# Edge pass of a graph network kernel: sixteen unread products a step in an unused PSUM bank

## The reference, cut to what matters

```
gate = silu(edge_attr @ F1W + F1b) @ F2W + F2b
ei = emb[atom_z[src]]
ej = emb[atom_z[dst]]
gate = gate + (ei * (ej @ adapt)).sum(-1, keepdims=True)
cw = where(distances < CUT, 0.5 * (cos(pi * distances / CUT) + 1.0), 0.0)
mj = node_mult[dst]
msg = gate * h[dst] * (cw * mj)[:, None]
agg = segment_sum(msg, src, num_segments=N)
tot = clip(segment_sum(mj, src, num_segments=N), 1e-08, None)
```

## Time and profile before

| | us |
|---|---|
| median of 3 runs | 19432.3 |
| the profiled execution: its time | 19381.23 |
| its span | 19379.5 |
| PE busy / DVE busy / POOL busy / ACT busy | 10513.3 / 11231.2 / 9046.0 / 5238.7 |
| mean granted TensorE clock, share of full | 0.687 |
| edge pass, from the first gather to the last partial sum | 2563 to 6381 |

### The profile page before, as it was taken

How to read it: one execution, slowest core, us unless ns; L and a number is a source line. 1 busy time by engine, 2 the same in 40 slices (tenths; PEclk the granted TensorE clock), 3 DMA queues, 4 the chain that set the end, 5 groups by cost and what they waited for, 6 DMA issues and landing times. The chain is left out here.

```text
span 19379.5 us, 403631 instructions
## 1 busy us (share of the span) xinstructions
PE 10513.3 (54%) x119643; PEld 7960.3 (41%) x119643; DVE 11231.2 (58%) x26717; ACT 5238.7 (27%) x15775; POOL 9046.0 (47%) x10645
## 2 busy tenths in 40 slices
PE   1001046666666327875894796588255555534334
PEld 1001024444444116864784786578233333333213
DVE  6557034454444456885887788588433333366647
ACT  0000012222222004652562464266122222211110
POOL 7778654444444533431441343244355545465251
PEclk9855555555555559997997998899566666655556
DMA  4552334443445217544552754555111111134434
GB/s 131 175 179 75 97 75 73 73 73 73 73 73 73 48 29 236 162 131 158 163 164 76 225 164 108 193 160 163 38 45 41 44 42 43 39 107 140 132 119 153
DMA packets 1580320, 2116.07 MB, mean 109 GB/s; under 512 B 418326, under 2 KB 1234222, under 8 KB 1573225
## 3 DMA queue, kind: packets, MB, share of 16 engines
q1 hardware_dynamic: 1196382, 1438.64, 24.0%
q0 software_dynamic: 309216, 539.49, 14.7%
q10 hardware_dynamic: 74552, 135.95, 2.1%
HBM read 1290.57 MB, written 726.03 MB: 104 GB/s over the span
## 5 line engine op out<-in xcount | busy, mean ns | idle before, releaser
L686 POOL DMA_INDIRECT attend_rows<-key_rows,attend_fetch_now x1824 | 1752.9, 961 | 2331.7 <-PE attend_seg L1722 2003.6
L686 POOL DMA_INDIRECT edges_rows<-raw,edges_perm_now x1824 | 1764.8, 968 | 2008.2 <-issue 1635.7
L1766 ACT ACTIVATE attend_hot<-attend_lane_hot,attend_share 128x128 f32<-128x128 fp8e4 x7296 | 2227.2, 387 | 114.0 <-DVE attend_share L1789 74.0
L686 POOL DMA_INDIRECT mlp_xin<-table,mlp_staged x1564 | 1492.3, 954 | 1441.4 <-PEq L2313 981.0
L686 POOL DMA_INDIRECT keys_rows<-table,keys_staged x1564 | 1867.9, 1194 | 539.4 <-issue 539.4
L1722 PE MATMUL attend_seg<-attend_rows,attend_hot 128*128 128x49 f32 x14592 | 1839.7, 280 | 81.4 <-issue 43.5
L1722 PEld LDWEIGHTS attend_seg<-attend_rows,attend_hot 128*128 128x128 f32 x14592 | 1763.7, 197 | 126.8 <-issue 119.9
L1709 PE MATMUL attend_qx<-attend_table,attend_oht 128*128 128x90 bf16 x21888 | 1106.4, 208 | 412.9 <-DMA attend_oht<-src_hots 361.6
L692 POOL DMA_INDIRECT messages<-spread_out,spread_place_now x912 | 1013.0, 1111 | 606.4 <-issue 470.3
L1709 PEld LDWEIGHTS attend_qx<-attend_table,attend_oht 128*128 128x128 fp8e4 x21888 | 1010.4, 101 | 479.8 <-issue 477.9
L1806 DVE TENSOR_REDUCE attend_mraw<-attend_top 128x2 f32<-128x1024 f32 x912 | 1110.3, 1217 | 52.2 <-issue 28.7
(11 more groups left out here) (546 smaller groups left out, 23345.9 us busy)
## 6 DMA issues: line engine op xcount, KB each, us to landing
key_rows<-expand_out SPq DMA_DIRECT2D x304, 624.0 KB
attend_ea<-edge_attrs SPq DMA_DIRECT2D x912, 160.0 KB
tally_rows<-messages SPq DMA_DIRECT2D x152, 864.0 KB, 4.8
attend_table<-q SPq DMA_DIRECT2D x1832, 67.5 KB
expand_oht<-dst_hots SPq DMA_DIRECT2D x304, 384.0 KB
attend_oht<-src_hots SPq DMA_DIRECT2D x912, 128.0 KB
attend_lane_hot<-src_hots_by_edge SPq DMA_DIRECT2D x912, 128.0 KB
raw<-keys_rows ACTq DMA_DIRECT2D x46, 2176.0 KB
```

The costliest lines, as they stand in the source:

```text
L686: return nc.gpsimd.indirect_dma_start(out=out, out_offset=None, in_=table, in_offset=bass.IndirectOffsetOnAxis(ap=index, axis=0))
L1766: ins = nc.scalar.activation(hot[p][:, u, c, :], lane_hot8[r][:, u, c, :], ACT.Copy, scale=share[p][:, u, c:c + 1])
```

## The change

It takes the eighth PSUM bank as `ps_idle` and defines `keep_busy`, which issues BUSY = 4 products of the identity in bf16 (128x128) with 512 columns of the embedding table (bf16, 128 partitions) into that bank, each overwriting the last. It is called behind L1093, L1101, L1119 and L1125, after the group's semaphore has been attached to its last product. Nothing reads the bank, no wait is added, and no other engine's stream differs.

```diff
+    BUSY = 4
...
-        ps_e2 = ph.ps("ps_e", [P, 512])
+        ps_e2, ps_idle = ph.ps("ps_e", [P, 512]), ph.ps("ps_idle", [P, 512])
...
+            def keep_busy():
+                for _ in range(BUSY):
+                    mm(ps_idle[:], k.identb[:], k.emb3[:, 0, 0:512], start=True, stop=True)
...
                             ins = nc.tensor.transpose(ps_t[0:RBF, u, c * P:(c + 1) * P], attr[p][:, u, c * RBF:(c + 1) * RBF], k.ident[:])
                     ins.then_inc(s_t, 1)
+                    keep_busy()
...
                                      start=(c == 0), stop=(c == GR - 1))
                     ins.then_inc(s_seg, 1)
+                    keep_busy()
...
                                 ins = mm(ps_e[:, u, c * G:(c + 1) * G], oht8[1 - p][:, u, c::GR], table[1 - p][:, u, j, :], start=(j == 0), stop=(j == 2))
                     ins.then_inc(s_exp, 1)
+                    keep_busy()
...
                         ins = mm(ps_1[0:F, u, :], w1[:], eT[:, u, :], start=True, stop=True)
                     ins.then_inc(s_1, 1)
+                    keep_busy()
```

## The result

The changed kernel takes **19522.7 us** (median of 6 runs, 19498.0 to 19564.6), the kernel before 19430.1 (6 runs, 19406.1 to 19483.6): ratio **1.0049**, 95% interval 1.0033 to 1.0065. It is 93 us slower. The profiled execution took 19528.8 us, its span 19527.1.

A forecast was written before the change was run, and what follows sets the result against it. POOL's gathers and PE's held signal were taken to bound the edge step; +22 us over 224 steps and +8 for last and first steps made +30, 19411 on the execution, 19460 on the median; range 19330 to 19720.

The forecast's parts named there:

- rival 1: Edge pass: PE becomes the bound through its added time and late L1125; 19500 to 19660, or 19840; chance 0.33.
- second push: PE holds only so much unreported behind held signals; 32 more instruction records a step bring one-at-a-time products nearer; no size.
- The ring of 16.54 us: Edge step: dot, 4.97 us through DVE to first gather, 9.95 of gathers, 1.62 until PE's signal is through.
- (a): Four products behind L1093, in PE's 3.22 us gap before L1101: cost nothing while L1093 starts early enough.
- (b): Four behind L1101 push L1110 and L1119 by 1.71 us: cost nothing, 2.2 us of cover left.
- (c): Four each behind L1119 and L1125: L1125 ends 3.2 us into the next step, L1101 starts at 8.8 instead of 7.13.
- One stretch of high clock a step: PE in the edge pass gets 3.4 us at the high clock each step, giving back 2 to 3 us.
- the crawl: PE's products come out one or two at a time; seen at L1119 in first steps, with 2.05 us idling before.
- The last steps: Three final edge steps without gathers: the four behind L1101 show in full, 3 x 1.7 = 5 us.
- first push: PE's time in the edge pass, 18.3 us a step against 16.5, if the clock gives back less than 1.8.
- Rival 2: Edge pass: L1119's signal gets out early in 5 to 25% of steps, -60 to -285 us; chance 0.20.
- the hold: The time in an edge step, while POOL gathers, when PE's signals reach other engines late; through 1.62 us after the last gather.

The follow-up runs named there:

- before_again: The kernel before, unchanged, profiled on the same chip as some of the experiments: 19446.8 us in one run, pass 3763.3 us.
- half_gathers: The kernel before with four gathers a step instead of eight from the edge pass's fifth step, waits matched: ratio 0.9454, pass 2713.2 us.
- gap_seven: The kernel before plus seven 512-column products behind the transposes alone, none elsewhere: ratio 1.0013, pass 3813.0 us.
- seg_sixteen_narrow: The kernel before plus sixteen 32-column products behind the segment sum alone: ratio 1.0042, pass 3855.4 us.
- narrow: The changed kernel with each of its sixteen added products 32 columns wide instead of 512: ratio 1.0018, pass 3847.0 us.
- after_again: The changed kernel again, profiled on one chip with the kernel before: ratio 1.0045, pass 3849.6 us.
- gate_first_early_oht: The kernel before with PE's second gate layer ahead of the segment sum and DVE's one-hot ahead of the row list, no added products: ratio 0.9960.
- narrow_again: The changed kernel with 32-column products instead of 512, repeated on a chip where the kernel before takes about 16775 us: ratio 1.0037.

## Why the prediction came out as it did

The range (19330 to 19720) held the time. The forecast, no change at 19460, did not: it is slower by 0.49%, the prediction's rival 1 (chance 0.33), and by that rival's second push. That the range held is in part luck: its upper side was priced for PE becoming the bound, which did not happen, and the mechanism that did act had no price.

1. *The ring of 16.54 us is POOL's gathers and the delay of PE's signal.* Right: before_again repeats it to 0.01 us a step, and half_gathers removes it.
2. *(a) Four behind the transposes: nothing.* Not shown: gap_seven, with seven there alone, has a pass 50 us longer than before_again, with 57 dots behind the expansion, but on another chip and with a ratio of 1.0013 whose interval reaches 1.
3. *(b) Four behind the segment sum: nothing, 2.2 us of cover left.* **This is the step that failed.** In time the cover was real: at its usual 0.77 us the expansion would have been over at 4511.15 + 0.77, +13.9, before the +14.3 that the text had and well before +16.5. But PE's earliness in time isn't cover for more instructions ahead of the expansion: with as few as before, all 24 products ran at once; with some more, most of them (14 and 15 in the steps shown) are left until 1.4 to 1.5 us after the last gather's end, run in 0.55 us, and the dot waits for them: 2.02 us behind the gather instead of 1.62, the 0.4 us a step of the loss. seg_sixteen_narrow shows the whole loss with 0.64 us of PE time.
4. *(c) L1125 ends at +3.2 of the next step, L1093 starts at +5.1, L1101 at 8.8.* The direction right, the size short: L1133 ended 5.25 us after the dot (4514.98) and the segment sum started at 4507.75, +9.7. The cause is again the crawl, since L1133 starts only when the last products of the expansion are out (4516.58). Likely it cost nothing by itself: in narrow the segment sum starts at +7.4 and the pass is as long.
5. *One stretch of high clock a step, of 3.4 us.* Right that it comes, and half its length: 0.70 in the earlier trace rows's window, inside the 0.6 to 0.8 named, is (0.70 - 0.50) / 0.50 of a step of 16.9 us, some 6.8 us at the high level, where 3.4 us would give 0.60. L1107 and L1117 are the ones that gained (0.70 us for 1.16, 1.98 for 3.65). So PE got more back than the sum allowed and was further from being the bound, and the step grew all the same.
6. *The last steps, +5 us for three.* Too dear: the three steps without gathers took 12.90, 11.30 and 13.96 us, 38.2 in all, against 37.9 before (6335.1 to 6373.1 us by the dots); in after_again they took 39.2.

```profile
6420.73 0.42 DVE L1220 TENSOR_TENSOR edges_dot<-edges_ps_e,edges_rows 128x256 f32<-128x256 f32 x1 [7.16 <-PE edges_ps_e L1126]
6433.63 0.42 DVE L1220 TENSOR_TENSOR edges_dot<-edges_ps_e,edges_rows 128x256 f32<-128x256 f32 x1 [3.46 <-PE edges_ps_e L1126]
6444.93 0.42 DVE L1220 TENSOR_TENSOR edges_dot<-edges_ps_e,edges_rows 128x256 f32<-128x256 f32 x1 [1.81 <-PE edges_ps_e L1126]
6458.89 0.42 DVE L1220 TENSOR_TENSOR edges_dot<-edges_ps_e,edges_rows 128x256 f32<-128x256 f32 x1 [6.32 <-PE edges_ps_e L1126]
```

   The middle step, at a granted clock of 1.00 from 6434 to 6445 us, gained 1.4 us where one without gathers was 12.73; in the last L1117 took 3.65 us again and the step lost as much. The middle one is what the Trainium skill, TensorE: Matmul & The Clock Gate, Part 1, would have: the array is throttled by default and activity releases it. Where PE is in the ring that pays; in 224 of 228 steps it isn't in the ring.
7. *The sum.* The term for the 224 steps was +0.1 us each, +22; it measured 0.38 a step, 86 us in all, against a measured 93 (64 to 126 by the interval).
8. *Rival 1, first push (PE's time, steps of 17 to 18.3 us, last gather over 2 us back).* Its sign of dots following L1119 at once appeared in all 228 steps, and the gather is 2.02 back, on the edge of what the text gave as the mark, while the step of 16.93 lies between the marks of "right" (16.5 to 16.8) and of "slow" (17 to 18.3); but narrow and seg_sixteen_narrow exclude PE's time. The second push, with the crawl of the earlier trace rows, is what the runs bear out; it was named and not priced apart.
9. *Rival 2 (the signal gets out before the hold).* It needed a signal that is over at +11.5 to get out, with the hold beginning at +11.8. gate_first_early_oht shows an expansion over at +9.2 caught in most steps. The reading of the earlier trace rows, where L1110's signal passed at +11.8, put the beginning too late: that step was one of the few in which a signal still passes so long after the first gather (19 in before_again).

## What to carry to other kernels

An engine that waits 4 us every step isn't free for more work if what it waits for is the delivery of its own signals: count instructions between the start of such a hold and the signal that matters, not their microseconds. Products added to raise TensorE's clock pay only where TensorE is in the ring that sets the step; look first at which wait ends last with the engine's work taken out, as the steps without gathers did here. And run the kernel before, with a profile, on the chip of each experiment: two of the four numbered chips here had no hold, and the same edit meant something else on them.

## What the runs showed of the hardware

- While POOL issues indirect gathers, PE's signals are delivered late on two of the four numbered chips (15 and 14) and on that of the first comparison: the expansion's signal 7.3 us after its product's end in gate_first_early_oht, whose gate layer's signal 2.45 us after the first gather still took 0.04. The hold is over about 1.4 us after the last gather's end (PE goes on at +1.43 in the change's step), and the dot followed at +1.62 before the change. That agrees with the Trainium skill, Perfetto Trace Analysis, section DMA Instruction - SWDGE (GPSIMD), only so far that work goes on behind the shown end of a gather. That another engine's signals wait for it was read from these runs alone.
- During the hold PE goes on for a while and then runs one or two products at a time, 0.5 to 1.2 us of idling before each, with "issue" as the reason for its waiting, which fits a limit on instructions that are finished and not reported. The limit's size was not measured, and that PE gets its next instructions late would look the same in these rows; no run separates the two.
- On two chips (7 and 3) there is no hold at all: signals take 0.03 to 0.04 us among gathers of the same 0.94 us, the dots follow PE, and the kernel before takes 16775 and 16779 us instead of 19430. What makes the chips differ stays open.
- PE's clock reacts within a step: L1117 ran in 2.00 us in one step of narrow_again and in 3.65 in the next.
